# A graph network in one kernel: the weighted edge passes with VectorE's loop written out and products of four rows at a time

## The reference

```
out = segment_sum(h_src * attn[..., None], dst)                 # layer 1, 8 heads of 32
out = segment_sum(att[:, :, None] * h[src], dst, n)             # layer 2, twice, 4 heads of 64
```

## Time and profile before

| | us |
|---|---|
| median of 3 runs | 4060.08 (4056.94 to 4063.56) |
| profiled execution, span | 5649.1 |
| PE, PEld busy | 3213.5, 1917.1 |
| DVE busy | 2171.3 |
| ACT busy | 1527.5 |
| POOL busy | 2057.0 |

### The profile page before, as it was taken

How to read it: one execution, slowest core, us unless ns; L and a number is a source line. 1 busy time by engine, 2 the same in 40 slices (tenths; PEclk the granted TensorE clock), 3 DMA queues, 4 the chain that set the end, 5 groups by cost and what they waited for, 6 DMA issues and landing times. The chain is left out here.

```text
span 5649.1 us, 65353 instructions
## 1 busy us (share of the span) xinstructions
PE 3213.5 (57%) x16684; PEld 1917.1 (34%) x16685; DVE 2171.3 (38%) x5425; ACT 1527.5 (27%) x3235; POOL 2057.0 (36%) x2082
## 2 busy tenths in 40 slices
PE   2111233349849965446802654771744464999998
PEld 1111111115537743223701522341522233444444
DVE  5222100001239884447301744780654458121213
ACT  0133200000349953234200032460033345121212
POOL 4665677750030045562174055306045641000000
PEclk5555555559979976667755866895866676999999
DMA  9323410014345632222412511004622231313231
GB/s 377 110 92 96 112 34 25 25 51 130 113 118 149 147 95 82 83 86 94 180 32 60 148 21 21 12 6 138 186 59 81 84 107 57 107 60 107 61 106 42
DMA packets 327831, 522.03 MB, mean 92 GB/s; under 512 B 141885, under 2 KB 203030, under 8 KB 323956
## 3 DMA queue, kind: packets, MB, share of 16 engines
q1 hardware_dynamic: 214361, 306.27, 18.4%
q0 software_dynamic: 78896, 124.49, 8.4%
q10 hardware_dynamic: 34381, 89.16, 4.2%
HBM read 407.66 MB, written 115.58 MB: 93 GB/s over the span
## 5 line engine op out<-in xcount | busy, mean ns | idle before, releaser
L1042 PE MATMUL ps<-shared_sb,onehot 128*128 128x264 f32 (+1 forms) x1600 | 600.2, 493 | 385.0 <-issue 217.5
L2100 DVE TENSOR_TENSOR accum<-accum,ps 128x264 f32 (+1 forms) x1248 | 529.4, 424 | 536.7 <-issue 311.9
L1327 ACT ACTIVATE onehot<-iota,drel 128x128 f32<-128x128 f32 x1248 | 381.3, 388 | 1068.6 <-PE ps L965 701.2
L1102 PE MATMUL ps<-score_sb,shared_sb 128*128 128x512 f16 (+1 forms) x3150 | 629.2, 360 | 20.6 <-DVE shared_sb L2129 20.2
L682 POOL DMA_INDIRECT score_sb<-table,idx_a x192 | 200.7, 1045 | 944.9 <-issue 465.3
L1042 PEld LDWEIGHTS ps<-shared_sb,onehot 128*128 128x128 f32 x1600 | 316.5, 230 | 670.9 <-issue 606.7
L812 PE MATMUL ps<-resid_sb,shared_sb 128*128 128x512 f32 (+1 forms) x416 | 297.1, 803 | 371.0 <-issue 318.5
L642 POOL DMA_INDIRECT t_w<-early_sb x391 | 389.4, 996 | 284.4 <-DVE counts L1836 182.3
L682 POOL DMA_INDIRECT shared_sb<-table,idx_a x384 | 364.1, 948 | 250.7 <-ACT idx_a L1310 140.0
L659 POOL DMA_INDIRECT t_adj<-counts,early_sb x391 | 403.6, 1032 | 121.5 <-issue 121.5
L1102 PEld LDWEIGHTS ps<-score_sb,shared_sb 128*128 128x128 bf16 x3150 | 298.6, 99 | 343.5 <-DVE shared_sb L2129 14.7
(11 more groups left out here) (413 smaller groups left out, 5592.3 us busy)
## 6 DMA issues: line engine op xcount, KB each, us to landing
score_sb<-t_adj SPq DMA_DIRECT2D x105, 640.0 KB, 3.9
accum<-t_hot SPq DMA_DIRECT2D x208, 256.0 KB
t_w<-accum ACTq DMA_DIRECT2D x13, 3200.0 KB
t_hot<-shared_sb SPq DMA_DIRECT2D x104, 256.0 KB
resid_sb<-t_w SPq DMA_DIRECT2D x25, 1024.0 KB
shared_sb<-t_key SPq DMA_DIRECT2D x98, 256.0 KB
t_adj<-accum ACTq DMA_DIRECT2D x35, 640.0 KB
shared_sb<-t_adj SPq DMA_DIRECT2D x35, 640.0 KB, 9.1
```

Of the source, the lines that this page charges most:

```text
L1042: pe.matmul(ps[:, RING[(HU * h + u) % len(RING)], 0:w], onehot[:, h % 2 * HU + u, :], around[g][place(g, i, h)][:, u, 0:w], start=True, st ...
L1102: mm = pe.matmul(ps[:, 2 * (i % 3) + f, 0:w], h_gin[:, t, m, f * P:(f + 1) * P], ring["gin"][:, at % HOLD, c, 0:w], start=(t == 0 and m == ...
L1327: last = act.activation(onehot[:, h % 2 * HU + u, :], iota[:, 0:P], ACT.Abs, bias=drel[:, bass.ds(step + u, 1)], scale=-1.0)
L2100: dve.tensor_tensor(to, to, bank.unsqueeze(1), ALU.add).then_inc(step_acc, 1)
```

## The change

VectorE's part of a pass is written out for all 52 octets: no loop, so that waits compare with constants and tile numbers are read at fixed places. `weigh(n, half)` multiplies four rows of octet n in one instruction and raises `msg_ready` by four. `add(n)` loads the eight tile numbers, snaps all of them at once, and then does its eight additions; the first half of the next octet is weighed ahead of addition 1, the second ahead of addition 5. Only the additions of even steps wait for `step_mm`, and then for the product of the next step too. Each addition still waits for the one before it. The fold of pass 1 comes behind octet 26.

```diff
             def add_up(g, w, H):
-                def weigh(i, h, u):
...
-                    v = around[g][place(g, i, h)][:, u, 0:D].rearrange("p (h d) -> p h d", h=H)
-                    of_src = v if g != 1 else x_rows[h][:, u, :].unsqueeze(1).to_broadcast([P, H, DX])
-                    dve.tensor_tensor(v, of_src, now_w[:, u, 0:H].unsqueeze(2).to_broadcast([P, H, D // H]), ALU.mult).then_inc(msg_ready, 1)
-
-                def add(i, h, ahead=None):
-
-                    step = RG[g] * i + HU * h
-                    dve.load(tn_regs, tn_i[0:1, bass.ds(step, HU)])
+
+                lap = RG[g] // HU
+                turns = S // HU
+
+                def buffer_of(n):
+
+                    return place(g, LAPS[g], n % lap) if n // lap == LAPS[g] else n % lap
+
+                def weigh(n, half):
+
+                    now = slice(half * GU, half * GU + GU)
+                    if half == 0:
+                        dve.wait_ge(w_ready, turns * g + n + 1)
+                    dve.wait_ge(*landed(g, 0, 2 * n + half))
+                    now_w = ps[:, 5 + n % lap % 2, 0:HU * 8].rearrange("p (u c) -> p u c", u=HU)
+                    v = around[g][buffer_of(n)][:, now, 0:D].rearrange("p u (h d) -> p u h d", h=H)
+                    of_src = v if g != 1 else x_rows[n % lap][:, now, :].unsqueeze(2).to_broadcast([P, GU, H, DX])
+                    dve.tensor_tensor(v, of_src, now_w[:, now, 0:H].unsqueeze(3).to_broadcast([P, GU, H, D // H]), ALU.mult).then_inc(msg_ready, GU)
+
+                def add(n):
+
+                    dve.load(tn_regs, tn_i[0:1, HU * n:HU * n + HU])
+                    tiles = [dve.snap(r, min_val=0, max_val=NT - 1) for r in tn_regs]
                     for u in range(HU):
-                        if ahead is not None:
-                            weigh(*ahead, u)
-                        at = dve.snap(tn_regs[u], min_val=0, max_val=NT - 1)
-                        dve.wait_ge(step_mm, S * g + step + u + RS + 1)
-                        dve.wait_ge(step_acc, S * g + step + u + len(RING))
-                        bank = ps[:, RING[(HU * h + u) % len(RING)], 0:w]
-                        to = accum[:, bass.ds(at, 1), 0:w]
+                        if u % GU == 1 and n + 1 < turns:
+                            weigh(n + 1, u // GU)
+                        dve.wait_ge(step_acc, S * g + HU * n + u + len(RING))
+                        to = accum[:, bass.ds(tiles[u], 1), 0:w]
+                        if u % 2 == 0:
+                            dve.wait_ge(step_mm, S * g + HU * n + u + RS + 2)
+                        bank = ps[:, RING[(HU * (n % lap) + u) % len(RING)], 0:w]
                         dve.tensor_tensor(to, to, bank.unsqueeze(1), ALU.add).then_inc(step_acc, 1)
...
-                with dve.Fori(0, LAPS[g] - 1) as i:
...
-                for h in range(LEFT[g]):
-                    add(LAPS[g], h, (LAPS[g], h + 1) if h < LEFT[g] - 1 else None)
+                for n in range(turns):
+                    add(n)
+                    if g == 1 and n == 26:
+                        fold(2, 4, P, (2, 3), "L2_gnn_a_src2", "L2_gnn_a_dst2", "ld_gat2")
                 dve.wait_ge(step_acc, S * (g + 1) + len(RING))
```

More of the change, by code:

```diff
@@ L2100, in add @@
                         dve.tensor_tensor(to, to, bank.unsqueeze(1), ALU.add).then_inc(step_acc, 1)
-                lap = RG[g] // HU
-                for u in range(HU):
-                    weigh(0, 0, u)
+                weigh(0, 0)
+                weigh(0, 1)
                 if g > 0:
```

## The result

The changed kernel takes 4066.90 us (median of 15 runs, 4058.58 to 4075.42) against 4058.46 us before (15 runs), a ratio of 1.0022 with a 95% interval of 1.0015 to 1.0029: 8 us slower. I forecast 4230 us. The sign was the likeliest one, the size wrong by a factor of twenty, and the time lies inside the range only because the range reached to the rivals. The price of an octet came out right; how much of it shows did not, and that anything shows at all hangs on some 10 us of pass 1 for which my sum had no term.

A forecast was written before the change was run, and what follows sets the result against it. VectorE was taken to set the pace of all three passes: +1.13 us an octet times 52, less 2 us, is 57 us a pass, 171 us in all, 4060 + 171 = 4231, said as 4230 us; range 4045 to 4290.

The forecast's parts named there:

- The price of an octet: VectorE's time for eight steps of a pass rises from 5.73 to 6.86 us, +1.13 us.
- R1: Gathers 1.25 us apart hold passes 0 and 2, hiding VectorE's extra; pass 1 pays 57 us: 4117 us; chance 0.2.
- R3: All three passes wait for gathers or their landing, pass 1 through a slower start: no change, 4060 us; chance 0.09.
- (a) to (c): VectorE, per octet: four-row products save 0.40 us; five uncovered addition pairs add 1.23; a7 to a0 takes 1.0.
- (d): Fewer waits and loop counters on VectorE's sequencer, hidden behind operations: counted at nothing beyond the additions' shorter spacing.
- (e): Written out instead of looped, three branches in pass 0, one in pass 1, three in pass 2 go: under 5 us.
- the low and high bounds of the sum: Octets of 6.34 us (+95 us in all) or 7.26 us (+235 us), from bounds on addition spacing and load gap.
- The rule of the skill: Next operation waits for an empty pipe, semaphores cost nothing extra: five addition pairs at 0.43 us each, near 4115 us.
- R2: The starved sequencer is the kernel's own and the written-out form needs it less: 60 us net gained, 4000 us; chance 0.17.
- R4: TensorE falls back to half clock: up to 84 us more, 4315 us; included in the 0.54 for all passes paying.
- TensorE's 93 halves in 40 us: After pass 1's gathers end, TensorE's half products in 40 us should fall from 112 to about 93.
- the sign named against me: The prediction is wrong if GpSimd never waits for ScalarE's indices in passes 0 and 2.

## Why the prediction was wrong

**What bounds the kernel: the step that failed.** The prediction set aside the stalls as "mostly the profiled execution's own" and put the passes at VectorE's 5.73 us an octet. The second holds, nearly, in the runs with few gathers alone (5.9 to 6.0 us). In the kernel as it is, GpSimd issues a gather every 1.25 us in the profiles from both kinds of chip, and runs without a profile take as long as those with one. The stream doesn't fit under VectorE: passes 0 and 2 take 412 us, not 298. I had this number from the earlier trace rows and had worked out R1 from it (320 x 1.25 = 400 us), but gave it 0.2, because "the 1589 us that the runs don't have can hardly be found without a shorter pitch". They were found without one: the pitch is the same, the passes are shorter (418, 353 and 419 us where the earlier trace rows has 604, 496 and 587), and the stages ahead and between are shorter by still more. The first load of pass 0 came at 2092.0 us in the stalled trace and at 1348.7 us in the other. I took a duration that had been steady throughout a disturbed trace for part of the disturbance.

**Pass 1.** R1 made it pay 57 us in any case, counting 192 of 416 gathers done at its start. That count was from the stalled trace. Where the stage before it isn't stalled, VectorE begins with 143 gathers issued:

```profile
L722 POOL DMA_INDIRECT resid_sb<-table,src_x x96: 942/947/1036, 1910.2 to 2029.2; - x96
L722 POOL DMA_INDIRECT shared_sb<-table,src_x x47: 942/947/2845, 2030.5 to 2095.1; - x47
```

(GpSimd's gathers of pass 1 until 2096 us, where VectorE's first load is; kernel before, 4060-chip.) The other 273 take 273 x 1.25 = 341 us, over VectorE's 300 and under its 357: of the 57 us some 10 stick out. That is R3's mechanism ("pass 1 too, through a slower start"), which I gave 0.09, and its 4060 us was nearest. It was not quite the whole: it said no change, and 8 to 12 us are measured. That pass 1 is the place is shown by the form with products of one row there alone: 1.0000 of the kernel before.

**(a) to (e).** (a) to (c) are right, as the octet of 6.87 us shows, and (d) cost nothing that can be seen. The sum of 171 us measured 146 and 153 where nothing hides it, because the kernel before is slower in passes 0 and 2 than I had it. My 5.73 us came from one octet of pass 1. The trace of the kernel before on a 4060-chip has in pass 0, at two loads of tile numbers:

```profile
1402.89 0.42 DVE L2086 TENSOR_TENSOR score_sb<-score_sb,ps 128x256 f32<-128x256 f32 x1 [0.41 <-issue]
...
1424.03 0.42 DVE L2086 TENSOR_TENSOR resid_sb<-resid_sb,ps 128x256 f32<-128x256 f32 x1 [3.59 <-issue]
```

The first is an ordinary load: 0.41 us where I had 0.28. The second stands behind the loop's branch (at 1420.1 us): when the loop goes round VectorE is idle for 3.5 to 3.8 us, though the branch itself takes 0.063. It goes round twice in pass 0, twice in pass 2 and never in pass 1. In the 4060-chip run with few gathers these four gaps are 3.69, 3.53, 3.54 and 3.57 us, 13 us more than four gaps of 0.28. The other gaps of passes 0 and 2 there are together 9 us longer than those of pass 1. That is 22 of the 25 us between 171 and 146. So (e), "under 5 us in all", was mis-sized: it is some 13 us. (With its own 2 us a pass taken off, the low and high bounds of the sum would be +89 and +233 us, not +95 and +235.)

**The rule of the skill.** By "The DRAIN you can't avoid" (the Trainium skill, VectorE: DVE Perf Modes) a semaphore between two operations costs nothing extra. In this kernel it does: 0.57 us from addition to addition with one wait and 0.63 to 0.65 with two and a register move, for an operation of 0.43 us. The 0.34 us between a product and an addition, which the prediction set against the page as well, is not at odds with it: the same section says that a next operation that is not held starts earlier. The near 4115 us that the rule gave is closer to the result than mine, but not by its reason.

**R2, faster.** It is what happens on 5640-chips, by 24 us instead of 60. Its reason fits in part: there the written-out form with single rows gains 54 us, and four rows in a loop lose 67. That it gains by having fewer register operations is argued, not shown. On 4060-chips there are no such stalls to save. **R4** did not come: TensorE's granted clock in the passes is higher after (0.90, 0.98, 0.88) than before (0.83, 0.92, 0.85), in the two tables by stage, each of another 4060-chip. VectorE's list of waits in pass 1 after the change names TensorE, but by its count it is the gap at the load:

```profile
DVE accum L2107 <- PE ps L1042: 33.0, 51, 1.0
```

33.0/51 is 0.65 us, one for each octet, as in the octet shown. It is filled by VectorE's own load (0.60 us) and its snaps (0.19 us), which begin with the last addition; TensorE has nothing to do with it.

**Signs.** Octets of 6.9 us and additions 0.6 us apart came true. So did TensorE's 93 halves in 40 us, already under the last gathers of pass 1, since VectorE waits for none of them (the changed kernel, as the earlier trace rows):

```profile
2380.00:2420.00 40.00, 28.44 (x93) 13.95 (x94) 31.88 (x60) 22.13 (x64) 30.20 (x33) 1.00 0.12 27
```

So, all but two waits of 0.3 us, did the sign named against me, "if GpSimd never waits for ScalarE's indices in passes 0 and 2": GpSimd's list of waits in pass 0 of the kernel before, on a 4060-chip, has

```profile
POOL shared_sb L682 <- ACT idx_a L1310: 0.6, 2, 0.3
```

and on the 5640-chip

```profile
POOL shared_sb L682 <- ACT idx_a L1310: 58.8, 10, 22.4
```

so the ring there was full at the stalled pace of the other engines, and told nothing of the pace without stalls.

## A version that is no worse anywhere

The written-out form with products of one row is level with the kernel before on a 4060-chip (1.0002) and faster on the 5640-chips (0.9908, 0.9903); it is also 0.2 to 0.3% under the change on the first and 0.5% on the second, by the ratios above. It beats the kernel before on the second kind alone.

## What to carry to other kernels

Merging small operations that alternate with a chain of waiting ones takes away the cover under which the waits ran: by the sum, which the octet bears out, 0.40 us saved an octet and 1.5 us uncovered. Before an engine is taken as the bound, lay beside it each stream that feeds it, at its own steady pitch times its count, in the stage in question; a pitch that holds through a disturbed trace is to be believed, and how far that stream is ahead at the stage's start isn't to be read from such a trace. And where a profile is 39% longer than the runs, ask for a second one before arguing from either.

## What the runs showed of the hardware

Three chips gave 5634 to 5655 us for the kernel before and three others 4059 to 4073 us (medians), with the same program, and no chip gave both. Each chip was measured in one stretch of time only, so that the level belongs to the chip is likely and not shown. On a 5640-chip other engines are held for microseconds at a time while GpSimd issues indirect DMAs. The changed kernel's pass 0 there, VectorE and then GpSimd:

```profile
2307.84 0.42 DVE L2107 TENSOR_TENSOR accum<-accum,ps 128x265 f32 x1
2316.17 1.01 DVE L2107 TENSOR_TENSOR accum<-accum,ps 128x265 f32 x2 [7.91 <-remote]
...
2311.95 0.94 POOL L682 DMA_INDIRECT shared_sb<-table,idx_a  x1 [0.30 <-issue]
2317.17 0.94 POOL L682 DMA_INDIRECT shared_sb<-table,idx_a  x1 [4.28 <-ACT idx_a L1310]
```

GpSimd's gathers run on at 1.25 us until 2312.89 us; then it has no more indices. VectorE goes on 3.3 us behind that, and ScalarE, which makes the indices, resumed at the same moment (2316.08). In the looped form register operations are slow there too, which I take for the same stalls. VectorE's at one line of the kernel before, first on a 5640-chip, then on a 4060-chip (ns min/median/max):

```profile
L2095 DVEq MOVE  x672: 3/36/726, 2541.1 to 4703.4; - x168
```

```profile
L2095 DVEq MOVE  x672: 36/36/43, 1610.8 to 3136.1; - x168
```

What differs between the chips, and why four more increments ahead of each gather take 5% off there, stays open. The gap of 3.5 to 3.8 us behind a branch that goes back was read on 4060-chips; its cause was not tested either.
